# A fused adaLN attention block on Trainium2: where the QKV stage rotates and splits, and where the last chunk's halves are written

## The reference, cut to what matters

```python
h = _layernorm(x, axis=-1) * (1 + ca) + sa
qkv = h @ W_qkv + b_qkv                     # per head q, k, v of 32
q = _apply_rope(q, cos, sin)                # r0 = x0*c - x1*s ; r1 = x0*s + x1*c
k = _apply_rope(k, cos, sin)
att = softmax(where(causal, q @ k.T / sqrt(32), -1e9))
x = x + ga * ((att @ v) @ W_proj + b_proj)
h = _layernorm(x, axis=-1) * (1 + cb) + sb
```

## Time and profile before

| what | us |
|---|---|
| median of 3 runs | 3386.67 (3384.64 to 3388.11) |
| profiled execution, its own time | 3387.18 |
| its span on the core | 3385.4 |
| PE busy | 3043.3 (90%) |
| DVE busy | 2615.7 (77%) |
| ACT busy | 1756.1 (52%) |
| POOL busy | 1780.8 (53%) |

### The profile page before, as it was taken

How to read it: one execution, slowest core, us unless ns; L and a number is a source line. 1 busy time by engine, 2 the same in 40 slices (tenths; PEclk the granted TensorE clock), 3 DMA queues, 4 the chain that set the end, 5 groups by cost and what they waited for, 6 DMA issues and landing times.

```text
span 3385.4 us, 59145 instructions
## 1 busy us (share of the span) xinstructions
PE 3043.3 (90%) x21664; PEld 1165.7 (34%) x21664; DVE 2615.7 (77%) x4326; ACT 1756.1 (52%) x3411; POOL 1780.8 (53%) x1617
## 2 busy tenths in 40 slices
PE   3799999889989999989998999999898999999895
PEld 1323333424343332424333243433424333242221
DVE  4687777897768788797877878788786878878577
ACT  3416565655655554665545555565544555555551
POOL 2404444473536656473664736566473655736454
PEclk8769999999999999999999999999999999999997
DMA  5302020312031120312103031221313112021122
GB/s 207 101 12 63 16 69 14 95 41 71 17 95 44 43 69 31 97 45 77 45 28 111 29 92 32 62 63 29 98 32 107 32 45 80 26 76 44 40 80 69
DMA packets 180875, 205.27 MB, mean 61 GB/s; under 512 B 21460, under 2 KB 137428, under 8 KB 179428
## 3 DMA queue, kind: packets, MB, share of 16 engines
q1 hardware_dynamic: 180584, 201.50, 20.6%
HBM read 114.09 MB, written 36.50 MB: 44 GB/s over the span
## 4 chain that ended last, share of the span: by engine, by line
PE 43%; DVE 22%; issue 12%; POOL 6%; ACT 6%; DVEq 5%; POOLq 5%; DMA 2%; SPq 1%; ACTq 0%
DVE mpart L873 10%; PE ring L1113 9%; PE ps_out L1163 9%; PE ps_scores L1149 7%; PE ps_den L1180 4%; PE ps_scores L1087 4%; PE ps_den L1186 3%; PE ring L1135 3%; POOL psum L511 2%; ACT xw L661 2%; DVEq L843 2%; DVE half L850 2%; DVE dsum L889 2%; ACT xr L663 2%; POOL psum L510 2%
## 5 line engine op out<-in xcount | busy, mean ns | idle before, releaser
L713 ACT ACTIVATE prob<-ps_scores 128x512 f32<-128x512 f32 (+3 forms) x2560 | 1263.5, 536 | 1096.0 <-PE ps_scores L1152 520.7
L873 DVE TENSOR_REDUCE mpart<-ring 128x1 f32<-128x512 f32 (+3 forms) x2560 | 1401.4, 599 | 303.3 <-PE ring L1116 150.3
L1149 PE MATMUL ps_scores<-qk 98*128 98x512 f16 (+3 forms) x2560 | 880.7, 358 | 102.0 <-DVE v L855 50.0
L1113 PE MATMUL ring<-qk 96*128 96x512 f16 (+3 forms) x2560 | 882.9, 367 | 74.6 <-DVE mpart L873 64.0
L510 POOL TENSOR_TENSOR psum<-prob 128x512 f32<-128x512 f32 x360 | 483.7, 1344 | 281.9 <-ACT prob L713 161.7
L1163 PE MATMUL ps_out<-prob,v 128*32 128x512 f32 (+3 forms) x5120 | 610.9, 549 | 0.0
L1113 PEld LDWEIGHTS ring<-qk 96*128 96x128 f16 x2560 | 238.7, 99 | 895.7 <-DVE mpart L873 640.2
L496 POOL TENSOR_TENSOR xw<-xw,turn 128x512 f32<-128x512 f32 x128 | 202.2, 1580 | 582.6 <-ACT xr L663 546.7
L511 POOL TENSOR_TENSOR psum<-prob 128x512 f32<-128x512 f32 x360 | 483.2, 1342 | 0.0
L1149 PEld LDWEIGHTS ps_scores<-qk 98*128 98x128 f16 x2560 | 249.8, 100 | 419.1 <-ACT prob L713 207.3
L1087 PE MATMUL ps_scores<-hT,wg 128*128 128x512 f16 x1536 | 346.1, 382 | 3.5 <-POOL hT L501 3.5
(11 more groups left out here) (122 smaller groups left out, 2557.6 us busy)
## 6 DMA issues: line engine op xcount, KB each, us to landing
qk<-half SPq DMA_DIRECT2D x384, 128.0 KB, 3.2
turn<-in_rope_dram SPq DMA_DIRECT2D x64, 512.0 KB, 4.2
xs<-in_L_attn_x_dram SPq DMA_DIRECT2D x124, 256.0 KB, 2.8
attn_out_T<-ot SPq DMA_DIRECT2D x63, 256.0 KB, 2.1
otin<-attn_out_T SPq DMA_DIRECT2D x30, 512.0 KB, 4.7
out_dram<-x SPq DMA_DIRECT2D x60, 256.0 KB, 2.1
wg<-w_qkv_halves SPq DMA_DIRECT2D x16, 768.0 KB, 5.4
qk<-in_L_wmod_dram SPq DMA_DIRECT2D x1, 6144.0 KB, 26.7
```

What stands on the lines that cost most here:

```text
L713: act.activation(prob[:, s % 3, p, h % 2, 0:w], ps_scores[(HG * s + h) % NBK][:, 0:w], ACT.Exp, scale=SCALE).then_inc(exp_done, 1)
L873: dve.tensor_reduce(mpart[:, h, qt, kc:kc + 1], ring[n % NBK][:, 0:w], AX.X, ALU.max).then_inc(ring_free, 1)
L1113: mm = pe.matmul(ring[n % NBK][:, 0:w], qk[0:R, G % 2, 0, h, qt * P:(qt + 1) * P], qk[0:R, G % 2, 1, h, kc * QC:kc * QC + w], start=True, ...
L1149: mm = pe.matmul(ps_scores[k % NBK][:, 0:w], qk[0:RM, par, 1, h, kt * P:(kt + 1) * P], qk[0:RM, par, 0, h, cq * QC + q0:(cq + 1) * QC], st ...
```

## The change

GpSimd's `sines` and `sin_done` go. VectorE's `cosines` becomes `turned_parts`, which multiplies `xw` by the sines and `xr` by the cosines and drains; the sum follows. In chunks 0 to 2 VectorE runs parts, sum, parts, sum, `leave_v`, `low`, `low`; in the last chunk `leave_v` comes after the first sum, and the two `low` move: into steps 0 and 1 of the main part, behind the first two row maxima of each (for the first QKV stage, which has no main part behind it, they stay at its end). ScalarE runs both `leave_qk` of a chunk and then both `high` of the same chunk; the last chunk's `high` move into step 0 of the main part, behind the exponentials of the second and the fourth head. SP's and TensorE's programs are the same.

```diff
-            def sines(G, c, kind):
-                j = job(G, c, kind)
-                S = NC_ * G + c
-                pool.wait_ge(turn_ld[S % 2], 16 * (S // 2 + 1))
-                pool.wait_ge(x_evac, j + 1)
-                pool.tensor_tensor(xw[:, j % 2, :], xw[:, j % 2, :], turn[:, S % 2, 1, :], ALU.mult).then_inc(sin_done, 1)
...
             def qkv(G, g, before):
                 for c in range(NC_):
                     leave_qk(G, g, c, 0)
-                    if c > 0:
-                        high(G, c - 1, 1)
                     leave_qk(G, g, c, 1)
                     if c == 0 and before is not None:
                         maxima(before)
-                    high(G, c, 0)
-                high(G, NC_ - 1, 1)
+                    if c < NC_ - 1:
+                        for kind in range(2):
+                            high(G, c, kind)
...
                             act.activation(prob[:, s % 3, p, h % 2, 0:w], ps_scores[(HG * s + h) % NBK][:, 0:w], ACT.Exp,
                                            scale=SCALE).then_inc(exp_done, 1)
+                            if s == 0 and h % 2 == 1 and nxt:
+                                high(G + 1, NC_ - 1, h // 2)
...
-            def cosines(G, c, kind):
+            def turned_parts(G, c, kind):
                 j = job(G, c, kind)
                 S = NC_ * G + c
                 dve.wait_ge(turn_ld[S % 2], 16 * (S // 2 + 1))
                 dve.wait_ge(x_evac, j + 1)
+                dve.tensor_tensor(xw[:, j % 2, :], xw[:, j % 2, :], turn[:, S % 2, 1, :], ALU.mult)
                 dve.tensor_tensor(xr[:, j % 2, :], xr[:, j % 2, :], turn[:, S % 2, 0, :], ALU.mult)
+                dve.drain()
...
             def qkv(G):
                 for c in range(NC_):
-                    cosines(G, c, 0)
+                    turned_parts(G, c, 0)
                     turned_sum(G, c, 0)
-                    cosines(G, c, 1)
-                    low(G, c, 0)
+                    if c == NC_ - 1:
+                        leave_v(G, c)
+                    turned_parts(G, c, 1)
                     turned_sum(G, c, 1)
-                    leave_v(G, c)
-                    low(G, c, 1)
+                    if c < NC_ - 1:
+                        leave_v(G, c)
+                        for kind in range(2):
+                            low(G, c, kind)
...
+                        if s < 2 and nxt:
+                            low(G + 1, NC_ - 1, s)
```

More of the change, by code:

```diff
@@ L233, in adaln_block_kernel @@
             sem(n) for n in ("head_stat", "head_rstd", "head_norm", "head_scaled", "head_hi", "head_done"))
-        qk_mm, v_mm, x_evac, v_evac, sin_done, turned, hi_done, lo_done = (
-            sem(n) for n in ("qk_mm", "v_mm", "x_evac", "v_evac", "sin_done", "turned", "hi_done", "lo_done"))
+        qk_mm, v_mm, x_evac, v_evac, turned, hi_done, lo_done = (
+            sem(n) for n in ("qk_mm", "v_mm", "x_evac", "v_evac", "turned", "hi_done", "lo_done"))
         turn_ld = [sem(f"turn_ld{i}") for i in range(2)]
@@ L565, in _ @@
                     head_low(0, t - 1)
-            for c in range(NC_):
-                for kind in range(2):
-                    sines(0, c, kind)
             for par in range(2):
@@ L581, in body @@
                     nxt = not (last and g == NG - 1)
[L582 to L585, removed]
                     pool.drain()
@@ L690, in _ @@
             qkv(0, 0, None)
+            for kind in range(2):
+                high(0, NC_ - 1, kind)
             def body(b, first, last):
@@ L838, in cosines @@
                 dve.wait_ge(x_evac, j + 1)
+                dve.tensor_tensor(xw[:, j % 2, :], xw[:, j % 2, :], turn[:, S % 2, 1, :], ALU.mult)
                 dve.tensor_tensor(xr[:, j % 2, :], xr[:, j % 2, :], turn[:, S % 2, 0, :], ALU.mult)
+                dve.drain()
             def turned_sum(G, c, kind):
                 j = job(G, c, kind)
-                dve.drain()
-                dve.wait_ge(sin_done, j + 1)
                 dve.tensor_tensor(xr[:, j % 2, :], xr[:, j % 2, :], xw[:, j % 2, :], ALU.add).then_inc(turned, 1)
@@ L969, in _ @@
             qkv(0)
+            for kind in range(2):
+                low(0, NC_ - 1, kind)
             for u in range(NS):
```

## The result

The changed kernel takes 3327.31 us (median of 5 runs, 3323.93 to 3331.65) against 3386.67 of the kernel before (5 runs): a ratio of 0.9825, with a 95% interval of 0.9811 to 0.9839. The forecast was 3314 (3284 to 3346). The profiled execution took 3331.65 us, its span 3329.9.

The account below looks back on a forecast made before the run. TensorE was taken as the bound, losing about 6 us in each of 15 QKV stages to a ScalarE-VectorE loop. Terms 42.0 + 6.6 + 4.4 + 4.6 + 12.9 + 2.5 = 73.0 off 3387.2 gave 3314 us (3284 to 3346).

Parts of the forecast that it names:

- picture of the stage: QKV stage: with VectorE rotating alone, TensorE sets the pace, four chunks of 7.88 us, done at +31.7, third score +32.5.
- fourth groups: Two groups, fourth of a batch, bound just at the edge by the `otin` load: 2 x 2.2 = 4.4 us less.
- Clock at the start of the main part: Behind each QKV stage: gain 7.4 us with the clock kept, 6.5 with it lost; 7.0 taken.
- free groups: Six groups without a tail in step 2 take the full gain: 6 x 7.0 = 42.0 us less.
- The tail groups: Nine groups with a tail in step 2: its loads move only with the second lower half, 2.2 us earlier.
- first groups: Three groups, first of a batch, TensorE already waiting 3.52 us ahead of the projection for loads: 3 x 2.2 = 6.6 less.
- The sign that TensorE would stand ahead of the projection in all nine tail groups: Step 2: TensorE idle there several us more than before in those nine, and none in the six others.
- second groups: Three groups, second of a batch, only `xs` loaded; GpSimd's second add comes 4.3 us earlier: 3 x 4.3 = 12.9 less.
- Turn tables: Table loads in QKV chunks: no median cost, half a microsecond at worst; rival that they land late: 3329 us, chance 0.07.
- The loads don't hold: Rival: SP's loads land earlier with the rest, all 15 groups gain 7.0 us: 3279 us, chance 0.10.
- VectorE sets the pace of the first steps: Rival, main part: first maximum plus two lower halves count, 3.4 us gained in each of six groups: 3344 us, chance 0.15.
- nothing is left of it: Rival: main parts give back what the stage saved, as a later wait absorbs it: 3385 us, chance 0.03.

## Why the prediction was right, and what of it was wrong

The forecast of 3314 was 13 us below the median, inside its range. Its picture of the stage held. What it missed lies behind the stage, nearly all of it on one side: of the 17.5 us that the profiled execution gained less than forecast, 6.2 are in the two fourth groups, 4.6 in the second ones, 3.4 in the free ones, 2.0 ahead of the first stage, 1.4 in the third group of the last batch and 0.5 in the first ones; the first stage gave 0.6 more.

**The stage, right.** Forecast against measured: third score +32.5 and +32.5, first maximum +34.5 and +34.3, second lower half +37.1 and +36.7, weights issued +39.1 and +39.2, step 1's fourth exponential +36.9 (clock kept) and +36.9. TensorE became the stage's bound.

**Clock at the start of the main part.** I took 7.0 between 6.5 and 7.4. It was kept in the group shown; the first four free groups gave 6.6 to 7.4. The other two (5.8, 5.1) lost part of the clock for one piece of about 3.5 us at +36. Both also carry the head, the first layer norm of the next batch; but so does the group whose stage starts at 567.2, which gave 6.9, and with the loads ahead of the stack DMAs the same two are 189.6 and 190.5 us long, 7.4 and 6.7 less than before. So the loss comes in some executions of a head group and not in others (windows of the group whose stage starts at 1321.0):

```profile
1357.00:1360.50 3.50, 3.50 (x22) 0.74 (x20) 3.15 (x6) 1.02 (x3) 0.00 (x0) 0.57 0.75 156
```

Sum 38.6 for 42.0: a term of the right kind, 3.4 too large.

**The tail groups, where the step failed.** I moved the wait ahead of the projection by SP's 2.2 us and left the length of what follows as it was. I had priced the clock at the start of the main part, and not at this second gap. In the fourth groups the change itself makes it: the projection was due at +42 now, and `otin` still landed at +47.5. In the one shown above the clock stood at 0.52 for 6.3 us behind that wait.

The fourth groups were to be 4.4 shorter and are 1.8 longer; the run that kept TensorE busy gave back 3.2 and 3.9 of it with the loads as late as ever.

In the first groups the gap was there before the change. I had read one of them, with 3.52 us of waiting and a projection of 2.75 behind it, and let it stand for all three. The two others, whose stages start at 1761.2 and 2568.2, already paid with the clock:

```profile
1814.79 5.28 PE L1135 MATMUL ring<-wp,otin 128*128 128x512 f16 x12 [5.12 <-issue]
```

```profile
2621.32 5.05 PE L1135 MATMUL ring<-wp,otin 128*128 128x512 f16 x12 [3.94 <-issue]
```

In the changed kernel the same three wait for 8.65, 9.95 and 8.75 us and their projections take 4.07, 4.06 and 4.45; in the first:

```profile
975.90 4.07 PE L1130 MATMUL ring<-wp,otin 128*128 128x512 f16 x12 [8.65 <-issue]
```

One projection got 1.3 us longer and two got 1.2 and 0.6 shorter. That the first groups gave 6.1 of 6.6 is thus in part luck. The sign that TensorE would stand ahead of the projection in all nine tail groups, several us more than before, came in the first and the fourth groups; the third of the last batch waits for 1.54, and the second groups load no `otin` there and don't wait.

**The second groups** were to give 4.3 each and gave 2.4, 2.9 and 3.0. The chain of GpSimd's adds came out as drawn (first at +46.6, +45.9 and +47.0, second right behind it), but ScalarE waits for the normalisation behind them. In the kernel before that wait was never over 2.3 us (the view of waits: who waits for whom, us in total, times, longest):

```profile
ACT ot L743 <- POOL osum L516: 55.4, 43, 2.3
```

In the changed kernel it is 3.66, 3.01 and 4.08 in the three second groups; the first of them:

```profile
1176.91 0.62 ACT L731 CAST ot<-osum 128x512 f16<-128x512 f32 x1 [3.66 <-POOL osum L509]
```

and the clock falls in the 6.5 us behind it (in this group of the kernel before it was 1.00 from +45 to +90), the same omission:

```profile
1179.50:1186.00 6.50, 5.54 (x23) 1.30 (x25) 3.43 (x7) 4.01 (x9) 5.82 (x6) 0.54 0.53 161
```

The run with the weights later bears this out. There the first add of the same group comes 2.3 us earlier, the wait is 1.38 instead of 3.66, the clock stays full, and the group is 4.0 us shorter:

```profile
1172.67 0.62 ACT L731 CAST ot<-osum 128x512 f16<-128x512 f32 x1 [1.38 <-POOL osum L509]
```

```profile
1172.00:1186.00 14.00, 12.63 (x90) 4.09 (x89) 12.17 (x22) 10.35 (x20) 10.84 (x11) 1.00 0.25 77
```

**Turn tables.** Landing 4.6 us on the median, and VectorE waited for one 4 times, 6.4 us in all: 1.5 to 1.6 each, not the half microsecond that I had as the worst. In all four of these stages the third score comes at +32.5 as elsewhere, so that no wait of TensorE came of it. That rival fell.

**The other rivals.** "The loads don't hold" was wrong as a forecast of this kernel, and its price, 3279, is near what the kernel costs when they don't: 3272. That nearness is partly luck, since it took 7.0 for every group, and against the kernel before the first groups then gave 11.9, 14.0 and 11.7, the fourth 9.0 and 5.5, the second 5.5, 5.8 and 6.6. "VectorE sets the pace of the first steps" (3344) did not come: the free groups gave 5.1 to 7.4 and not 3.4. It was near all the same, as VectorE is busy for 5.03 of the first 5.10 us behind the stage. The rival "nothing is left of it" fell with the result. The profiled execution is 4 us above the median, inside the runs' own spread (3323.93 to 3331.65). The 2.0 us that it is later at the first stage I did not trace to a cause; the experiments reach theirs anywhere from 108.2 to 110.8 us, so that it can be the spread of single executions.

## What to carry to other kernels

When a stage in front is shortened, list for each engine's queue what the next stage wants first and by when, and what it is queued behind; a load that landed just in time before will be waited for now. Such a load belongs ahead of the waits that have no deadline. Price a wait of TensorE with the clock behind it: here 3.1 us of idling cost another 2.5 in the twelve matmuls that followed. Look at every group of a kind before one stands for all: the one that was read here had kept its clock, the two others had not.

## What the runs showed of the hardware that was not expected

- TensorE kept its full clock over 5.1 us in which it was busy for 4.0 (with 1.1 idle in one piece). In a stretch of 5.2 us in which it was busy for 2.09 and waited 3.11 in one piece, it lost it: the 6.3 us behind stood at 0.52.
- The length of a wait alone did not decide this. Behind waits of 2.11, 2.17 and 2.04 us in one run the same twelve matmuls took 4.43, 2.76 and 2.76; in the kernel before, behind 3.52, 3.94 and 5.12, they took 2.75, 5.05 and 5.28.
- 832 KB of another load issued ahead of a 512 KB one delayed its landing by about 1.8 us beyond the two issues (6.9 against 5.1 from issue to landing).
- Where both engines ran two-input operations on SBUF, VectorE's 0.69 became 1.64, beside additions of GpSimd that took 1.58 each (6.32 for four). How long these take alone no run shows. GpSimd's own multiplies in the kernel before took 1.26 us at the shortest and 1.77 in the median.
